# Taps products of four channels at a time, keys in every chunk, and pairs between the block products of a fused decoder layer

## The reference

```python
dt = jnp.exp(log_dt)
A = A_re + 1j * A_im
C = C_re + 1j * C_im
dtA = dt[:, None] * A
dC = C * (jnp.exp(dtA) - 1.0) / A
powers = jnp.exp(dtA[:, :, None] * jnp.arange(L))
K = 2.0 * jnp.einsum('dn,dnl->dl', dC, powers).real
```

```python
h = jnp.einsum('bsd,dh->bsh', x, W_exp) + b_exp
h = butterfly(h, up_weights, D_HIDDEN)
h = jax.nn.gelu(h + up_bias, approximate=False)
```

## Time and profile before

| | us |
|---|---|
| median of 3 runs (4576.86 to 4579.74) | 4579.71 |
| the profiled execution's own time | 4584.67 |
| its span, first to last instruction | 4583.1 |
| taps stage, in the span | 0 to 318.2 |
| folding stage, in the span | 318.2 to 463.0 |
| busy: PE 86%, PEld 71%, DVE 55%, POOL 44%, ACT 32% | |

### The profile page before, as it was taken

One profiled execution on the slowest core, in us unless ns is written; L12 is line 12 of the kernel. 1 busy time (PEld: TensorE's weight loads), 2 busy tenths in 40 slices (PEclk: granted clock), 3 DMA queues, 4 the chain that ended last, 5 costly groups with the idle time before them and its releaser, 6 DMA issues. The chain is left out here.

```text
span 4583.1 us, 63160 instructions
## 1 busy us (share of the span) xinstructions
PE 3961.9 (86%) x20956; PEld 3268.6 (71%) x20956; DVE 2529.4 (55%) x8674; ACT 1480.3 (32%) x2319; POOL 2030.0 (44%) x1411
## 2 busy tenths in 40 slices
PE   7866799958668888888799997959999999999998
PEld 4653678838667778777687775748877877778786
DVE  8615476568888888886456553224433345222222
ACT  3434354336456666665101002212111112111111
POOL 0000121137658777777465231026766765323332
PEclk9778899969889999999899998969999999999999
DMA  3343523320100101100543224341221232000000
GB/s 103 115 167 80 158 85 101 97 75 12 49 25 15 50 29 37 45 12 6 202 141 122 83 105 146 115 140 53 78 63 56 75 95 69 21 22 23 24 26 19
DMA packets 244943, 337.15 MB, mean 74 GB/s; under 512 B 66898, under 2 KB 125170, under 8 KB 241268
## 3 DMA queue, kind: packets, MB, share of 16 engines
q1 hardware_dynamic: 154868, 186.17, 13.6%
q10 hardware_dynamic: 87184, 138.46, 9.0%
q0 software_dynamic: 2560, 8.39, 0.5%
HBM read 220.70 MB, written 112.25 MB: 73 GB/s over the span
## 5 line engine op out<-in xcount | busy, mean ns | idle before, releaser
L2823 POOL TENSOR_TENSOR m_act_hl<-m_g,m_act_hl 128x512 fp32r<-128x512 f32 x256 | 355.5, 1389 | 679.1 <-DVE m_act_hl L3129 679.1
L1615 PE MATMUL xa_ps_t<-xa_diag,xa_s_buf 128*128 128x128 f32 x4096 | 525.1, 289 | 142.1 <-ACT xa_a L1702 74.8
L1615 PEld LDWEIGHTS xa_ps_t<-xa_diag,xa_s_buf 128*128 128x128 f32 x4096 | 512.7, 204 | 163.2 <-issue 80.8
L3129 DVE CAST m_act_hl<-m_g 128x512 fp32r<-128x512 f32 x256 | 139.4, 545 | 850.7 <-ACT m_g L2997 850.7
L1779 DVE MAX8 xa_cand<-xa_s_buf 128x8 f32<-128x64 f32 x4096 | 542.8, 218 | 65.5 <-ACT xa_s_buf L1665 39.7
L2997 ACT ACTIVATE m_g<-m_ps_h,m_b 128x512 f32<-128x512 f32 x256 | 176.2, 688 | 1116.5 <-PE m_ps_h L82 1111.4
L80 PE MATMUL m_ps_h<-m_hT,m_w 128*128 128x512 f32 x1024 | 417.3, 408 | 19.3 <-issue 17.2
L81 PE MATMUL m_ps_h<-m_hT,m_w 128*128 128x512 f32 x1024 | 409.4, 400 | 0.0
L82 PE MATMUL m_ps_h<-m_hT,m_w 128*128 128x512 f32 x1024 | 408.8, 399 | 0.0
L80 PE MATMUL m_ps_o<-m_w,m_act_hl 128*128 128x512 f32 x1024 | 406.8, 397 | 0.7 <-POOL m_act_hl L2823 0.7
L1543 POOL TENSOR_SCALAR xa_s_buf<-xa_s_buf,xa_top 128x1024 f32<-128x1024 f32 x120 | 344.3, 2870 | 141.0 <-ACT xa_prob L1684 141.0
(11 more groups left out here) (384 smaller groups left out, 8395.5 us busy)
## 6 DMA issues: line engine op xcount, KB each, us to landing
at_xk<-in_x_dram SPq DMA_DIRECT2D x128, 128.0 KB, 2.7
spectrum<-df_yo ACTq DMA_DIRECT2D x32, 512.0 KB, 2.8
id_raw<-spectrum SPq DMA_DIRECT2D x32, 512.0 KB, 5.6
m_xt<-x ACTq DMA_DIRECT2D x64, 256.0 KB, 4.0
tp_awT<-in_ctx_dram SPq DMA_DIRECT2D x16, 768.0 KB, 4.8
xa_ks<-kt SPq DMA_DIRECT2D x48, 256.0 KB
xa_raw<-in_ctx_dram SPq DMA_DIRECT2D x32, 384.0 KB, 3.4
kt<-tp_aw SPq DMA_DIRECT2D x4, 2048.0 KB, 8.9
```

The costliest lines, as they stand in the source:

```text
L1615: last = pe.matmul(ps_t[:, c // 4, c % 4, :], s_buf[:, t % 2, h, k0:k0 + P], diag[:, h, :], start=(h == 0 and c % 4 == 0), stop=(h == HEAD ...
L2823: pool.tensor_tensor(lo, g32[:, :], hi.bitcast(F32), ALU.subtract).then_inc(s_gl, 1)
```

## The change

- `taps(c)`: a product now takes four neighbouring channels at once, 4 x 32 = 128 weight columns and 128 moved columns, four products for a group instead of sixteen. Of the 16 blocks of 32 x 32 that come out, the four on the diagonal are taps and the rest is not used. `ps_k` has 128 partitions, and ACT takes a group out with four copies of 32 partitions x 128 elements instead of one of 512.
- `tabT[1]` is now laid out as [128, 128 channels, 32 steps], so that the weights are 128 neighbouring elements; ACT therefore writes its eight copies of a chunk with 128 bytes from one element to the next. `tabT[0]` stays, and is still read with 512 bytes from one element to the next.
- `key_groups(c)` stands in all four chunks, and `keys_stored(c)` stands in SP's queue after the contexts of the chunk and ahead of the store of its taps.
- In the folding stage the 16 bias products come first (new semaphore `s_mb`), then the 16 block products, and the value weights are turned after them. ACT and DVE do `partners(q)` and `pair(q)` of the first level as soon as blocks 2q and 2q+1 are copied. The copies of the film products start at pair 10 instead of pair 4.

```diff
@@ stage_taps, SP @@
                 for c in range(DC):
-                    if c >= 1:
-                        keys_stored(c - 1)
-                    if c < DC - 1:
-                        for g in range(KB * c, KB * (c + 1)):
+                    for g in range(KB * c, KB * (c + 1)):
+                        if g + 2 < KB * DC:
                             context(g + 2)
+                    keys_stored(c)
                     sp.wait_ge(s_kc, NG * (c + 1))
...
-                context(KB * DC - 2)
-                context(KB * DC - 1)
                 store(DC - 1)
-                keys_stored(DC - 1)
@@ taps(c), PE @@
-                        for q in range(G):
-                            d = g * G + q
-                            last = pe.matmul(ps_k[:, n % 2, q, :], tabT[1][:, :, d], tabT[0][:, :, d], start=True, stop=True)
+                        for q in range(4):
+                            d = slice(g * G + 4 * q, g * G + 4 * q + 4)
+                            last = pe.matmul(ps_k[:, n % 2, q, :, :], tabT[1][:, :, :].rearrange("p r d -> p (r d)")[:, R * (g * G + 4 * q):R * (g * G + 4 * q + 4)],
+                                             tabT[0][:, :, d].rearrange("p r d -> p d r"), start=True, stop=True)
@@ PE @@
                     turn(c, 0)
-                    if c < DC - 1:
-                        key_groups(c)
+                    key_groups(c)
                     turn(c, 1)
...
-                key_groups(DC - 1)
@@ ACT @@
-                        act.activation(tabT[i][:, 4 * g:4 * g + 4, :], ps_t[:, n % 2, :, :], ACT.Copy).then_inc(s_trc, 1)
+                        if i == 0:
+                            out = tabT[0][:, 4 * g:4 * g + 4, :]
+                        else:
+                            out = tabT[1][:, :, :].rearrange("p r d -> p (r d)").rearrange("p (d r) -> p r d", r=R)[:, 4 * g:4 * g + 4, :]
+                        act.activation(out, ps_t[:, n % 2, :, :], ACT.Copy).then_inc(s_trc, 1)
...
-                        act.activation(krow[:, g * G:(g + 1) * G, :], ps_k[:, g % 2, :, :], ACT.Copy).then_inc(s_kc, 1)
+                        channels = krow[:, g * G:(g + 1) * G, :].rearrange("r (q d) a -> r q d a", d=4)
+                        for d in range(4):
+                            last = act.activation(channels[:, :, d, :], ps_k[R * d:R * (d + 1), g % 2, :, d, :], ACT.Copy)
+                        last.then_inc(s_kc, 1)
@@ stage_butterfly, PE @@
+                pe.wait_ge(s_trc, 16)
+                pe.wait_ge(s_cup, 16 * 5)
+                pe.wait_ge(s_eu, 1)
+                for h in range(HC):
+                    last = pe.matmul(ps_b[:, h:h + 1], e_up[:, h * P:(h + 1) * P], wT[:, h, D:D + 1], start=True, stop=True)
+                last.then_inc(s_mb, 1)
+                for h in range(HC):
+                    if h >= 2:
+                        pe.wait_ge(s_mmc[h % 2], h // 2)
+                    pe.matmul(ps[:, h % 2, :], e_up[:, h * P:(h + 1) * P], wT[:, h, 0:D], start=True, stop=True).then_inc(s_mm, 1)
                 pe.wait_ge(s_wv, 32)
...
@@ ACT @@
-                for h in range(0, HC, 2):
-                    act.wait_ge(s_mm, h + 1)
-                    act.activation(wT[:, h, 0:D], ps[:, h % 2, :], ACT.Copy).then_inc(s_mmc[0], 1)
                 act.wait_ge(s_bias, 1)
-                for n in range(TOP * PAIRS):
+                for q in range(PAIRS):
+                    act.wait_ge(s_mm, 2 * q + 1)
+                    act.activation(wT[:, 2 * q, 0:D], ps[:, 0, :], ACT.Copy).then_inc(s_mmc[0], 1)
+                    act.wait_ge(s_mmc[0], q + 1)
+                    partners(q)
+                for n in range(PAIRS, TOP * PAIRS):
                     partners(n)
...
@@ DVE @@
+                dve.wait_ge(s_mb, 1)
+                dve.tensor_copy(wT[:, :, D:D + 1], ps_b[:, 0:HC].rearrange("p (h o) -> p h o", o=1))
+                dve.drain().then_inc(s_bias, 1)
+                for q in range(PAIRS):
+                    dve.wait_ge(s_mm, 2 * q + 2)
+                    dve.tensor_copy(wT[:, 2 * q + 1, 0:D], ps[:, 1, :])
+                    dve.drain().then_inc(s_mmc[1], 1)
+                    pair(q)
```

More of the change, by code:

```diff
@@ L127, in stage_taps @@
         ps_t = psum("ps_t", [P, 2, 4, P])
-        ps_k = psum("ps_k", [R, 2, G, R])
+        ps_k = psum("ps_k", [P, 2, 4, 4, R])
         ps_o = psum("ps_o", [P, 4, P])
@@ L400, in _ @@
                         i, g = n // 8, n % 8
-                        act.activation(tabT[i][:, 4 * g:4 * g + 4, :], ps_t[:, n % 2, :, :], ACT.Copy).then_inc(s_trc, 1)
-                        if n == 7 and c < DC - 1:
+                        if i == 0:
[3 more added lines that the diff above has]
+                        act.activation(out, ps_t[:, n % 2, :, :], ACT.Copy).then_inc(s_trc, 1)
+                        if n == 7:
                             key_groups(c)
@@ L655, in stage_butterfly @@
         s_trc = sem("transposed_copied")
+        s_mb = sem("bias_product")
         s_mm = sem("block_product")
@@ L747, in _ @@
                     last.then_inc(s_wvt, 1)
-                pe.wait_ge(s_trc, 16)
-                pe.wait_ge(s_cup, 16 * 5)
-                pe.wait_ge(s_eu, 1)
-                for h in range(HC):
-                    if h >= 2:
-                        pe.wait_ge(s_mmc[h % 2], h // 2)
-                    blk = e_up[:, h * P:(h + 1) * P]
-                    pe.matmul(ps_b[:, h:h + 1], blk, wT[:, h, D:D + 1], start=True, stop=True)
-                    pe.matmul(ps[:, h % 2, :], blk, wT[:, h, 0:D], start=True, stop=True).then_inc(s_mm, 1)
                 for n in range(2 * FILM):
@@ L797, in _ @@
                                    ACT.Copy).then_inc(s_trc, 1)
-                for h in range(0, HC, 2):
-                    act.wait_ge(s_mm, h + 1)
-                    act.activation(wT[:, h, 0:D], ps[:, h % 2, :], ACT.Copy).then_inc(s_mmc[0], 1)
                 act.wait_ge(s_bias, 1)
-                for n in range(TOP * PAIRS):
+                for q in range(PAIRS):
[4 more added lines that the diff above has]
+                for n in range(PAIRS, TOP * PAIRS):
                     partners(n)
-                    if n >= 4 and n % 2 == 0 and (n - 4) // 2 < 2 * FILM:
-                        film_copied((n - 4) // 2)
+                    if n >= PAIRS + 2 and (n - PAIRS - 2) % 2 == 0 and (n - PAIRS - 2) // 2 < 2 * FILM - 2:
+                        film_copied((n - PAIRS - 2) // 2)
+                for n in range(2 * FILM - 2, 2 * FILM):
+                    film_copied(n)
                 for n in range(0, 16, 2):
@@ L844, in _ @@
                        .then_inc(s_wvc, 1)
-                for h in range(1, HC, 2):
-                    dve.wait_ge(s_mm, h + 1)
-                    dve.tensor_copy(wT[:, h, 0:D], ps[:, h % 2, :]).then_inc(s_mmc[1], 1)
-                dve.wait_ge(s_mmc[0], HC // 2)
-                dve.tensor_copy(wT[:, :, D:D + 1], ps_b[:, 0:HC].rearrange("p (h o) -> p h o", o=1))
-                dve.drain().then_inc(s_bias, 1)
                 dve.wait_ge(s_ms, 16)
                 dve.tensor_scalar(mask[:, :], mask_u8[:, :], BIG, -BIG, ALU.mult, ALU.add).then_inc(s_mask, 1)
-                for n in range(TOP * PAIRS):
+                for n in range(PAIRS, TOP * PAIRS):
                     pair(n)
```

## The result

The changed kernel takes 4553.65 us, median of 5 runs (4548.83 to 4559.21), against 4579.71 (4576.86 to 4586.95, 5 runs): ratio 0.9942, 95% interval 0.9927 to 0.9956, so 20 to 33 us less. Its profiled execution took 4548.83 us, with a span of 4547.2 us and a mean granted clock of 0.944.

What follows compares the result with a forecast made beforehand. Most waits lie in the untouched last stage; in the first two, PE's products bound taps, and load, PE and DVE bound folding in turn. Taps 23.3 plus folding 4.5 makes 27.8 us less: 4579.71 to 4551.9, say 4552, range 4528 to 4568.

Steps and rivals of the forecast that it cites:

- A record of 0.225 us, a chunk of 14.4: Taps products on PE: spread operand priced at half speed, 4.3 us less a chunk, 12.9 us over chunks 1 to 3.
- fixed 0.022 us: Taps products: the part of the old 0.073 us a record taken as not depending on columns.
- (a): Taps products: pace was per instruction, spread reads free; 0.118 us a record, 7.6 us a chunk, 4531.5 us; chance 0.30.
- (b): Taps products: all a price per column, so products save nothing; 13.2 us less in all, 4566.5 us; chance 0.22.
- I take nothing: ACT's scattered copies into `tabT[1]`: no added cost, 0.597 us each; some 20 us kept as the other bound.
- rival (c): Copies into `tabT[1]`: writes also priced per access, 1.25 us each, 18.6 us lost; 4585.1 us with (b); chance 0.08.
- The queue in chunk 1: 7.6 us: SP's queue: chunk 1's context issued at about 131, no longer behind the keys' store, so PE passes 7.6 us earlier.
- Contexts in chunks 2 and 3 no longer waited for: 5.8 us: PE's waits of 3.60 us in chunk 2 and 2.22 us in the last keys vanish, their contexts being issued well before.
- The end of the stage: 3.0 us more: Taps stage's end: last keys, 24.7 us, now precede the last taps' way out and back, 18.4 us; 43.1 against 40.1.
- The folding stage: 4.5 us less: Folding stage: ACT's last result copy at 439.7 instead of 444.2, films being late next; bounds 1 and 8 us.
- Rival (d): Folding stage: bias products keep the clock low, films at that clock cost 4 us and give its gain back; 4556; chance 0.06.
- What ends the stage: Folding stage's end: store of `b`, issued at 444.21 behind ACT's last result copy; next stage starts 18.8 us later.

Runs made afterwards that it cites:

- e4: Changed kernel with `tabT[0]` also laid channel by channel, so both operands of the taps products are neighbouring and ACT scatters both tables' copies; 4543.57 us, ratio 0.9915.
- e11: Kernel before, its 32-column products and key order kept, with both tables laid channel by channel and copied with e6's walk; 4540.24 us, single run.
- e5: Changed kernel with `tabT[1]` copied plainly to neighbouring elements, so the taps are other numbers; 4553.55 us, single run.
- e6: Changed kernel with ACT's scattered copies walking the other way, for each channel its four rows, 16 bytes written together; 4551.15 us, ratio 0.9936.
- e9: Changed kernel with e8's bias store, e4's layout and e6's walk for both tables; 4520.9 us, ratio 0.9875.
- e12: e9 with the one-channel, 32-column taps products of before and ACT's one copy a group, on e11's neighbouring operands; 4522.3 us, ratio 0.9869.
- e3: Kernel before, its taps products and copies kept, with only the key groups in all four chunks and the keys' stores early; 4569.48 us, ratio 0.9975.
- e8: Changed kernel with the bias `b` turned on PE to 16 rows of 128 and its store issued after ACT's second result copy; 4544.04 us, ratio 0.9922.
- e7: Changed kernel with the unturned store of `b` issued after ACT's first result copy instead of its last; 4553.75 us, ratio 0.9935.

## Why the prediction was right, point by point

It said 4552 us and 27.8 us less; the medians say 4553.65 and 26.1. The total was right, but errors of opposite sign stand inside it: the slower copies, the waits left and the clock. That they cancel to 2 us is luck.

- **A record of 0.225 us, a chunk of 14.4.** It is 0.2225 and 14.24. The direction of the working holds: e4 reads the same columns from neighbouring elements in 0.128, so the spread operand costs 1.74 times as much, where my two rows gave 0.203 / 0.118 = 1.72. The fixed 0.022 us that I added is not borne out: e11's records of 32 columns take 0.032 in all, and 32 columns at the pace of 0.118 for 128 would be 0.030. That the sum of the two came within one per cent is partly luck. Rivals (a) and (b) fall. (a)'s price of some 0.12 us was there for whoever laid the operand out, but not its chunk of 7.6 us: ACT's four copies of a group take 1.11 us, where I had 0.8, and this, hidden behind the 1.78 us of PE here, holds e4 to 9.4.
- **"I take nothing" for ACT's copies into `tabT[1]`: the mis-sized term.** They took 1.07 us, not 0.597, and followed each other at some 0.91 us; rival (c) had 1.25 for that, and twice the loss in each chunk. I had argued that a copy at 1 ns an element is slower than any read in question and so would hide it; e5 and e6 show that the distance adds to the copy. From the start of `turn(c, 1)` to the first product it is 2.2 to 2.8 us more in each chunk. Chunk 0's share went into the wait for chunk 1's context, as the next point shows; the other three make 7.3 us, and 7.5 and 8.9 us came back in e5 and e6.
- **The queue in chunk 1: 7.6 us.** PE passed the point 143.83 - 137.45 = 6.4 us earlier: the context was issued at 132.35, not at 131. That SP's order decides there, and not the pace of the products, is right. The keys' store goes only when DVE has made the low keys, at 120.6 to 121.5 in the eleven profiles with the new places, and the taps' store behind its 2 MB lands late. e5, where chunk 0's taps are done 2.5 us sooner (SP's queue):

```profile
120.89 0.37 SPq L205 DMA_DIRECT2D kt<-tp_aw  x1
121.85 0.34 SPq L217 DMA_DIRECT2D tap_rows<-tp_krow  x1
131.60 0.34 SPq L221 DMA_DIRECT2D tp_kd<-tap_rows  x1
131.98 16.60 SPq L201 DMA_DIRECT2D tp_awT<-in_ctx_dram  x4
```

  The taps take 9.7 us to land instead of the changed kernel's 7.6, and PE passes the point at 137.39. In e9 and e12 the taps are done 7 to 9 us sooner, and PE still passes it at 137.41 and 136.93.
- **Contexts in chunks 2 and 3 no longer waited for: 5.8 us.** 2.0 us remain (0.56 + 1.45).
- **Not in the sum at all: the clock.** By the rows it made up for the copies. Windows of the kernel before, over chunk 1's products and the turning behind them (us, busy of PE, PEld, DVE, ACT, POOL, granted clock, DMA share, GB/s):

```profile
165.15:183.83 18.68, 18.68 (x257) 18.61 (x258) 16.57 (x32) 4.24 (x7) 0.00 (x0) 0.56 0.01 2
183.83:191.83 8.00, 7.16 (x33) 5.78 (x33) 0.00 (x0) 4.82 (x9) 0.00 (x0) 0.54 0.64 130
```

  The changed kernel, over the same work:

```profile
161.33:175.58 14.25, 14.25 (x66) 13.64 (x67) 12.91 (x29) 7.53 (x28) 0.00 (x0) 0.88 0.29 122
175.58:182.80 7.22, 5.15 (x40) 3.98 (x39) 3.63 (x4) 5.62 (x13) 0.00 (x0) 1.00 0.57 109
```

  And e3, with the old products in the new order of keys:

```profile
158.27:176.95 18.68, 18.68 (x257) 18.62 (x258) 17.20 (x33) 4.25 (x7) 0.00 (x0) 0.59 0.28 114
...
185.37:212.51 27.14, 21.73 (x106) 12.91 (x104) 18.75 (x34) 15.60 (x30) 0.30 (x1) 1.00 0.50 159
```

  During the old products the granted clock was mostly at its lower level, 1.2 GHz, and before it stayed there for the turning behind them; in the changed kernel that work runs at 1.00, which is 2.4 GHz. I had used to say that the products' own pace doesn't depend on the clock, and had not asked what runs next. Before, in the same chunk, both low stretches show as slow rows, the second behind the wait of 3.60 us at 202.82:

```profile
186.48 5.20 PE L257 MATMUL tp_ps_t<-tp_ident,tp_tab 128*128 128x128 f32 x24
...
204.58 4.58 PE L293 MATMUL tp_ps_q<-tp_awT,tp_aw 128*128 128x512 f32 x6
```

  The same six records take 2.81 us after (at 191.02, above). In e3 they do too, and all of its chunk from 185.37 on has the clock at 1.00: with the waits for contexts went the low clock behind them, so the part of this gain behind the waits belongs to the keys' new places. The part right behind the products belongs to them in part: in e3 the clock is 0.70 from 176.95 to 185.37, where it was 0.54 before and is 1.00 after. By such differences, waits for contexts apart, it comes to some 3.9 us from the end of chunk 1's products to `turn(2, 1)`, 1.5 behind chunk 2's products and 2.6 in the last keys (20 transposes in 4.27 us at 280.08), 8.0 in all, less 0.2 that chunk 1's keys lost after. No run held everything else fixed and changed only the clock: this is read from rows, not tested.
- **The end of the stage: 3.0 us more.** From the taps' store at 279.16 to the next stage it is 18.6 us, where I had 18.4; the store itself goes 1.2 us behind the last product (before 0.65), ACT's four copies standing ahead of it. The PE wait was 8.6 us for the 9 that I named. The 24.7 us for the last keys, though, were partly low clock, as above.
- **The folding stage: 4.5 us less.** 5.3 in the two profiles, 4.2 by the means. The bias products began 31.8 us after the start, where I had 32.4, and lasted 6.96 us, where I had 6.2. The films began at 65.4 and the store of `b` went out at 121.0, both as predicted. Rival (d), films at the lower clock, cost at most the 22.62 - 20.76 = 1.9 us by which their first half is slower than their second.
- **What ends the stage.** I named the store of `b` and its 18.8 us and left it at that; e8 shows that 10 us of it was the shape of that store.

For the first stage, 23.3 us were predicted and 20.4 profiled, 2.9 us less gained. From PE's rows of both kernels: copies in chunks 1 to 3 +7.3, contexts +2.0, chunk 1's queue +1.2, the end of the stage +0.8, products -0.7, and clock -7.7. No run showed one of these terms alone but the copies (e5, e6).

## What to carry to other kernels

Before merging instructions to pay a price fewer times, find out which price it is: here a changed layout gave more than the merge (a chunk in 8.3 us instead of 14.2) at no more work. A layout changed for a reader is paid by its writer, and here the writer's walk could be turned so that runs of 16 bytes are written, at no price. And where a small transfer lands late, count its packets before moving its issue: moved as it was it only held up the large ones (e7); turned into rows, for one transpose and a copy of 0.25 us, it landed in 2.9 us and the stage was 10 us shorter (e8).

## What was not expected of the hardware

- Float32 records with 32 columns go at 0.032 us from neighbouring elements and 0.073 us at 512 bytes' distance; with 128 columns it is 0.128 from neighbouring elements (granted clock 1.00) and 0.2225 when the moved operand alone is at that distance.
- A 128 x 512 copy on ScalarE from PSUM takes 0.60 us when it writes runs of 16 bytes 128 bytes apart while reading at 512 bytes' distance, and 1.07 us when it writes single elements 128 bytes apart.
- An 8 KB store as single elements lands after 12.1 to 14.6 us, and beside it a 256 KB store on the other queue kept its buffer for 12 us (e7); as 16 rows of 512 bytes the 8 KB land after 2.9.
- Behind products that lose nothing at the lower clock the turning ran at a granted clock of 0.54 before and 1.00 after; and behind a wait of 3.60 us the next projection took 4.58 us instead of 2.81. That the one makes the other is read from rows, not tested.
